# A decoder layer on one core: the first attention's sums turned in SBUF, GpSimd's bias work in pieces, stacks on every second partition

## The chip, the cores and the metric

The kernel runs on 1 core of a Trainium2 chip. The metric is the time of one execution on the device in microseconds (us).

## What is computed

The input is x, 16 batches of 128 tokens with 128 features, and a context of the same shape. Three blocks follow each other, each with a residual and a layer norm. Cut to what matters:

```python
# block 1: 16 heads of 8 features
scores = q @ k.T * SCALE                       # per head, 128x128
esc    = eq @ ek.T / sqrt(8) * exp(-0.1*|i-j|)  # the "entangled" scores
attn   = softmax(scores + 0.5 * esc)
ctx    = attn @ mixed                           # mixed: values with two gates
x = ln(x + ln(x + ctx @ Wo.T + bo) * g + b)
# block 2: cross attention on the context, 16 heads of 8, then layer norm
# block 3: 16 experts, top 4, GLU, then layer norm
```

## The kernel before

**Parts and stacks.** Projections are in float32. Each is split into three bfloat16 parts (`high`, `middle`, `lowest`; L1206 to L1217 on ScalarE, L494 to L506 on GpSimd, GpSimd forming the remainders). SyncE spills the parts of a batch to DRAM in five DMAs (`spill`, L348 to L374) and reads them back as stacks (`stack1`, L376 to L386; `stack2`, L388 to L397): a stack puts 6 parts times 8 features of every head on R = 48 partitions, so that one bfloat16 matmul over the 128 partitions of `stk` (the other rows are zeros from a memset at L484) sums all products of parts. `stack1` moves a batch in two halves of 8 heads, each half in one DMA.

**The first attention** goes in slots, one for each batch, with four units of four heads (g = 0 to 3) in a slot. In slot n the scores of batch n-1 are made, and the older batches n-2 to n-6 are at later steps; the remainders of batch n+2 are formed. TensorE's order in a unit is written out in `unit1` (L866): entangled scores (L753), at g = 1 and 3 the weighing of values (`weigh`, L838), the scores (L763), at g = 2 the projection of a later batch (L731), then for the unit before (lag 1) `subtract_max` (L768), for the one before that (lag 2) `turn` (L775), and at g = 1 `to_tokens` (L851).

One unit passes through these steps:

1. VectorE, `pick` (L1507): entangled scores times decay, PSUM to SBUF.
2. VectorE, `maximum` (L1517): four custom instructions add the picked scores to the scores, in place in PSUM (banks 0 and 1), and leave each row's maximum in `shift`.
3. TensorE, `subtract_max`: one 512-column bfloat16 matmul adds -shift to the bank.
4. ScalarE, `exponent` (L1219): exp, PSUM to `prob` in SBUF.
5. TensorE, `turn`: four float32 transposes of `prob` into bank 3.
6. ScalarE, `take_turned` (L1245): copy of bank 3 to `prob_t`.
7. TensorE, `weigh`.

**GpSimd** runs `slot1` (L582): `gain_and_sum` of batch n-5, the remainder of batch n+2, `inverse_root` for batch n-4, `mix_values` of batch n-1, `lowest` of batch n+2, `inverse_root` for batch n-5. Between the early slots it forms `xb_all` (x plus bo) and `xl_all` (x plus the norm's bias) in four additions each (`base`, L601, called at L619 to L628); VectorE waits for all four of `xb_all` at L1686, ahead of slot 4. Late in the first attention it forms the second block's `xb_all` in place (`residual_bias`, L636; 8, 4 and 4 batches).

**The overlap of the attentions.** From slot 14 on the projections and parts of the second attention are made (`begin2` on TensorE at L1007 and on ScalarE at L1375, `first_parts2` on GpSimd at L662), and from slot 17 the two attentions' units are interleaved until slot 20; then `slot2` runs alone. At (14, 0) ScalarE waits until the last spills of both buffers have landed (L1381).

**The start.** SyncE issues the weights, then `spill` and `stack1` of batches 0 and 1 with the load of `x_tok` (1 MB, L412) between the spill of batch 1 and its stack, then `late_w` and the further batches.

## Time and profile before

| | |
|---|---|
| median of 3 runs | 363.0 us (362.45 to 364.02) |
| the profiled execution's own time | 365.59 us |
| its span, first to last instruction | 363.8 us |
| mean granted clock of TensorE | 0.978 of full speed |
| first attention alone (slots 1 to 16) | about 18.9 to 159.5 us of the span |
| both attentions interleaved (slots 17 to 20) | to about 182 us |
| second attention alone | to about 265 us |
| experts and the last norm | to the end |
| busy shares | PE 91%, DVE 71%, ACT 60%, POOL 59% |
| DMA queue of SyncE | 67328 packets, 52.43 MB |

PE is TensorE's matmuls, PEld its weight loads, DVE is VectorE, ACT ScalarE, POOL GpSimd, SP SyncE; a letter q behind a name is its queue. Instructions overlap: the row of one gives its whole duration, while the next one on the same engine can start some 0.1 us before its end. So what one costs its engine is read from start to start.

### The profile page before, as it was taken

The numbers are of one execution on the slowest core, as the hardware profiler recorded it, in microseconds if no ns is written. First come the engines' busy times: TensorE is split into PE (matmuls) and PEld (weight loads), VectorE is DVE, ScalarE is ACT, GpSimd is POOL, SyncE is SP. The second block draws the span as 40 slices with busy tenths as digits, with TensorE's granted clock in tenths as the row PEclk, the third lists the DMA queues.
The fourth block names the chain that finished last, engine by engine and source line by source line (L and its number), as shares of the span: only waits on it lengthen the run. The fifth ranks groups of instructions, "written<-read, shape, count | busy, mean of one in ns | idle before, by whom it ended". The sixth has DMA issues, their size and how long they took to land.

```text
span 363.8 us, 11400 instructions
## 1 busy us (share of the span) xinstructions
PE 332.0 (91%) x3536; PEld 256.6 (71%) x3536; DVE 257.2 (71%) x1220; ACT 218.7 (60%) x522; POOL 215.0 (59%) x401
## 2 busy tenths in 40 slices
PE   8987989999999979896799999999799999999993
PEld 5766777877787758775678788888556765666662
DVE  1686888999999988875457776769945269345454
ACT  3785778999998866684586766756453252212120
POOL 8475789998888874876753334321125355464552
PEclk9998999999999998998899999999999999999998
DMA  7799899798998895947355757561046220444310
GB/s 232 174 304 239 220 235 238 177 208 200 196 208 186 208 204 107 255 95 150 76 126 106 156 127 140 126 138 46 2 136 202 77 60 0 142 128 131 128 32 29
DMA packets 67807, 54.06 MB, mean 149 GB/s; under 512 B 29616, under 2 KB 57648, under 8 KB 67632
## 3 DMA queue, kind: packets, MB, share of 16 engines
q1 hardware_dynamic: 67328, 52.43, 60.4%
q10 hardware_dynamic: 432, 1.05, 0.9%
q8 instruction: 24, 0.39, 0.5%
q14 instruction: 23, 0.19, 0.2%
HBM read 33.40 MB, written 20.05 MB: 147 GB/s over the span
## 4 chain that ended last, share of the span: by engine, by line
PE 51%; issue 13%; DVE 11%; ACT 9%; POOL 6%; DMA 5%; SPq 3%; ACTq 0%; POOLq 0%; DVEq 0%
PE bank L838 7%; PE bank L1106 5%; PE bank L1110 4%; PE bank L1119 4%; DMA parts_dram<-parts 3%; PE bank L792 3%; PE bank L821 3%; PE bank L814 3%; PE bank L731 3%; PE bank L781 3%; PE bank L763 2%; PE bank L771 2%; PE bank L851 2%; DMA stk<-parts_dram 2%; ACT parts L1217 2%
## 5 line engine op out<-in xcount | busy, mean ns | idle before, releaser
L1526 DVE CUSTOM_DVE_ANT_0 bank<-bank,decayed_e 128x128 f32<-128x128 f32 x256 | 67.2, 325 | 0.5
L697 POOL TENSOR_TENSOR stk<-stk 128x512 f32<-128x512 f32 x32 | 40.7, 1271 | 38.5 <-ACT stk L1442 35.8
L1537 DVE TENSOR_REDUCE top<-bank 128x4 bf16<-128x512 f32 x64 | 43.9, 687 | 19.5 <-PE bank L792 19.3
L1234 ACT ACTIVATE prob_t<-bank 128x512 f32<-128x512 f32 x64 | 38.8, 606 | 27.9 <-PE bank L821 27.6
L1442 ACT ACTIVATE stk<-bank 128x512 f32<-128x512 f32 x32 | 19.1, 597 | 53.6 <-PE bank L1106 53.6
L1781 DVE TENSOR_TENSOR stk<-bank,stk 128x512 f32<-128x512 f32 x32 | 22.0, 691 | 39.1 <-POOL stk L697 38.0
L1224 ACT ACTIVATE prob<-bank 128x512 f32<-128x512 f32 x64 | 39.2, 613 | 16.3 <-PE bank L771 16.0
L838 PE MATMUL bank<-prob_t,vmix 128*32 128x128 f32 x1024 | 43.6, 283 | 5.5 <-ACT pvs L1258 5.5
L1514 DVE TENSOR_TENSOR decayed_e<-bank,decay 128x512 f32<-128x512 f32 x64 | 44.0, 688 | 4.4 <-issue 4.3
L499 POOL TENSOR_TENSOR rest<-pf,parts 128x256 f32<-128x256 f32 (+1 forms) x31 | 28.1, 906 | 27.7 <-ACT parts L1213 27.7
L505 POOL TENSOR_TENSOR parts<-rest,parts 128x256 bf16<-128x256 f32 (+1 forms) x31 | 28.1, 906 | 25.9 <-ACT parts L1217 25.9
L781 PE MATMUL bank<-ident,prob 128*128 128x128 f32 x256 | 39.7, 279 | 0.0
L1250 ACT COPY prob_t<-bank 128x512 f32<-128x512 f32 x64 | 38.3, 599 | 0.9 <-PE bank L781 0.7
L1526 DVE DVE_READ_ACCUMULATOR2_ANT shift<- 128x1 bf16 x256 | 37.1, 145 | 0.1
L781 PEld LDWEIGHTS bank<-ident,prob 128*128 128x128 f32 x256 | 31.1, 143 | 6.5 <-issue 2.4
L838 PEld LDWEIGHTS bank<-prob_t,vmix 128*32 128x32 f32 x1024 | 26.4, 111 | 13.0 <-issue 7.8
L1119 PEld LDWEIGHTS bank<-w,stk 128*128 128x128 f32 x192 | 25.1, 191 | 11.9 <-issue 8.4
L1106 PE MATMUL bank<-x_t,w 128*128 128x512 f32 x64 | 32.8, 595 | 0.0
L1110 PE MATMUL bank<-x_t,w 128*128 128x512 f32 x64 | 32.7, 592 | 0.0
L753 PE MATMUL bank<-stk 128*128 128x128 bf16 x256 | 25.2, 222 | 3.4 <-DMA stk<-parts_dram 2.8
L763 PE MATMUL bank<-stk 128*128 128x128 bf16 x256 | 25.2, 221 | 2.3 <-ACT prob L1224 2.2
L771 PE MATMUL bank<-shift,neg_ident 128*128 128x512 bf16 x64 | 24.9, 389 | 2.1 <-DVE shift L1526 1.9
(172 smaller groups left out, 781.1 us busy)
## 6 DMA issues: line engine op xcount, KB each, us to landing
stk<-parts_dram SPq DMA_DIRECT2D x32, 384.0 KB, 5.4
stk<-shares_dram SPq DMA_DIRECT2D x64, 128.0 KB, 3.0
parts_dram<-parts SPq DMA_DIRECT2D x32, 192.0 KB, 3.1
parts_dram<-parts SPq DMA_DIRECT2D x48, 128.0 KB, 2.8
stk<-parts_dram SPq DMA_DIRECT2D x32, 192.0 KB, 3.5
parts_dram<-parts SPq DMA_DIRECT2D x32, 96.0 KB, 2.9
parts_dram<-parts SPq DMA_DIRECT2D x48, 64.0 KB, 2.1
w<-in_w_dram SPq DMA_DIRECT2D x3, 512.0 KB, 5.5
```

The source lines that it names most:

```text
L697: pool.tensor_tensor(h1[kk % 2], sg[kk % 2], share[kk], ALU.mult).then_inc(weighted, 1)
L781: t = pe.transpose(bank[3][:, 128 * j:128 * j + 128], prob[g % 2][:, j, :], ident[:])
L838: w = pe.matmul(bank[4][32 * j:32 * j + 32, 128 * m:128 * m + 128], vmix[b.par][:, head(2 * m, j) // 2, e:e + 2, :].rearrange("p e f -> p ...
L1106: pe.matmul(bank[kk % 2][:], w1[:, 128 * kk:128 * kk + 128], xt, start=True, stop=True).then_inc(gate_mm, 1)
L1110: pe.matmul(bank[UP_BANK[u % 3]][:], w3[:, 128 * kk:128 * kk + 128], xt, start=True, stop=True).then_inc(up_mm, 1)
L1119: m = pe.matmul(bank[4 + c % 2][:, 128 * t:128 * t + 128], actt[u % 3][:, 128 * t:128 * t + 128], w2[:, kk, :], start=(kk == 0 and t == 0) ...
L1224: act.activation(prob[g % 2][:].rearrange("p h t -> p (h t)"), bank[g % 2][:], ACT.Exp).then_inc(L.exped, 1)
L1234: act.activation(prob_t[g][:].rearrange("p h t -> p (h t)"), bank[2 + g % 2][:], ACT.Exp).then_inc(L2.exped, 1)
L1250: act.copy(prob_t[g][:].rearrange("p h t -> p (h t)"), bank[3][:]).then_inc(L.turned_ev, 1)
L1514: dve.tensor_tensor(decayed_e[:, g % 2], bank[E_BANK[g % 2]][:].rearrange("p (h t) -> p h t", h=GH), decay[:].unsqueeze(1).broadcast_to([1 ...
L1526: m = dve.tensor_tensor_reduce(out=bank[g % 2][:, 128 * j:128 * j + 128], in0=bank[g % 2][:, 128 * j:128 * j + 128], in1=decayed_e[:, g % ...
L1537: dve.tensor_reduce(top[:, b.par, GH * g:GH * g + GH], bank[S2_BANK[g % 2]][:].rearrange("p (h t) -> p h t", h=GH), AX.X, ALU.max).then_in ...
```

## The change

1. `maximum` writes its sums to SBUF (`sums`) and no longer back to the bank. `turn` transposes the sums (float32) into bank 3 and adds -shift there with four 128-column bfloat16 matmuls; it runs at lag 1. ScalarE's `exponent` reads bank 3 and writes `prob_t`. `subtract_max`, `take_turned` and `prob` are gone. Scores now wait for `maxed` and no longer for `exped`.
2. `residual_bias` goes in four pieces of 4 batches, and the parts of the second attention's first four batches are formed inside GpSimd's slots 14 to 17 (`last_slot1`). The `base` additions are spread over slots 2 to 7, and VectorE waits for the first of them ahead of slot 4 and for all four ahead of slot 6.
3. ScalarE's wait at (14, 0) for both spill buffers is replaced by one for the buffer in question ahead of `high` in slots 14 and 15. One wait of TensorE (L1078) is dropped.
4. The 48 rows of each stack lie on partitions 0, 2, ..., 94 in place of 0 to 47.
5. The load of `x_tok` is issued after both halves of batch 1's stack.

```diff
-        prob = [sb(f"prob{p}", [128, GH, S]) for p in range(2)]
+        sums = [sb(f"sums{p}", [128, GH, S]) for p in range(2)]
...
-                sp.dma_start(dst[0:R, :, at:at + H // 2], src[:, :, at:at + H // 2]
+                sp.dma_start(dst[0:2 * R:2, :, at:at + H // 2], src[:, :, at:at + H // 2]
...
-                    sp.dma_start(stk2[b.buf][0:R, side], src[side]).then_inc(L2.stacked[b.buf], 16)
+                    sp.dma_start(stk2[b.buf][0:2 * R:2, side], src[side]).then_inc(L2.stacked[b.buf], 16)
...
             spill(L1, Batch(0, 1))
-            sp.dma_start(x_tok[:].rearrange("p b n -> p (b n)"), k["x_tok"]).then_inc(in_xt, 16)
             sp.wait_ge(zeroed[1], 1)
             stack1(Batch(0, 1), 0)
             spill(L1, Batch(1, 0))
             stack1(Batch(0, 1), 1)
+            sp.dma_start(x_tok[:].rearrange("p b n -> p (b n)"), k["x_tok"]).then_inc(in_xt, 16)
...
+            pool.wait_ge(dve_set, DV_END)
+            slot1(1, 0)
             pool.wait_ge(in_tail_rows, 16)
             pool.wait_ge(in_xt, 16)
-            pool.wait_ge(dve_set, DV_END)
             base(xb_all, bo1, 0, base_x)
-            slot1(1, 0)
             base(xb_all, bo1, 1, base_x)
+            slot1(1, 1)
             base(xb_all, bo1, 2, base_x)
-            slot1(1, 1)
             base(xb_all, bo1, 3, base_x)
+            slot1(2, 0)
             base(xl_all, ln_b, 0, base_b)
-            slot1(2, 0)
-            for c in range(1, 4):
-                base(xl_all, ln_b, c, base_b)
+            pool.wait_ge(base_b, 1)
+            slot1(2, 1)
+            base(xl_all, ln_b, 1, base_b)
+            slot1(3, 0)
+            base(xl_all, ln_b, 2, base_b)
+            slot1(3, 1)
+            base(xl_all, ln_b, 3, base_b)
             pool.wait_ge(base_b, 4)
-            slot1(2, 1)
-            pair1(3)
...
+            def last_slot1(n, parts):
+
+                b = Batch(n // 2, n % 2)
+                if b.back(5).live:
+                    gain_and_sum(b.back(5))
+                if b.back(4).live:
+                    inverse_root(b.back(4), 0)
+                if parts is not None:
+                    remainder(L2, parts)
+                if b.back(1).live:
+                    mix_values(b.back(1))
+                if b.back(5).live:
+                    inverse_root(b.back(5), 1)
+                if parts is not None:
+                    lowest(L2, parts)
+
             pool.wait_ge(L1.low, NB)
-            first_parts2(0)
-            slot1(7, 1)
-            residual_bias(0, 8)
-            first_parts2(1)
-            slot1(8, 0)
-            first_parts2(2)
-            slot1(8, 1)
-            slot2(slot_batch(0))
-            slot1(9, 0)
+            for n in range(14, 17):
+                last_slot1(n, Batch2(0, n - 14))
+            last_slot1(17, Batch2(0, 3))
+            residual_bias(0, 4)
+            last_slot1(18, None)
             slot2(slot_batch(1))
+            residual_bias(4, 8)
+            last_slot1(19, None)
+            slot2(slot_batch(2))
             residual_bias(8, 12)
-            slot1(9, 1)
-            slot2(slot_batch(2))
-            slot1(10, 0)
+            last_slot1(20, None)
             slot2(slot_batch(3))
             residual_bias(12, NB)
...
-                    pe.wait_ge(L1.exped, u - 1)
+                    pe.wait_ge(L1.maxed, u - 1)
...
-            def subtract_max(b, g):
+            def turn(b, g):
+
                 u = b.n * NG + g
                 pe.wait_ge(L1.maxed, u + 1)
-                pe.matmul(bank[g % 2][:].rearrange("p (h t) -> p h t", h=GH), neg_ident[:],
-                          shift[:, g % 2, :].unsqueeze(2).broadcast_to([128, GH, S]),
-                          start=False, stop=True, skip_group_check=True).then_inc(L1.shifted, 1)
-
-            def turn(b, g):
-                u = b.n * NG + g
-                pe.wait_ge(L1.exped, u + 1)
                 if not isinstance(u, int) or u >= 1:
-                    pe.wait_ge(L1.turned_ev, u)
+                    pe.wait_ge(L1.exped, u)
                 for j in range(GH):
-                    t = pe.transpose(bank[3][:, 128 * j:128 * j + 128], prob[g % 2][:, j, :], ident[:])
-                t.then_inc(L1.turned, 1)
+                    pe.matmul(bank[3][:, 128 * j:128 * j + 128], sums[g % 2][:, j, :], ident[:], start=(j == 0), stop=True,
+                              is_transpose=True, skip_group_check=True)
+                for j in range(GH):
+                    m = pe.matmul(bank[3][:, 128 * j:128 * j + 128], shift[:, g % 2, j:j + 1].broadcast_to([128, 128]),
+                                  neg_ident[:], start=False, stop=True, skip_group_check=True)
+                m.then_inc(L1.turned, 1)
...
-                    if (n, g) == (NB + 1, 2):
-                        pe.wait_ge(L1.exped, NG * NB)
...
+            def exponent(b, g):
                 u = b.n * NG + g
-                act.wait_ge(L.shifted, u + 1)
-                if not isinstance(u, int) or u >= 2:
-                    act.wait_ge(L.turned, u - 1)
-                act.activation(prob[g % 2][:].rearrange("p h t -> p (h t)"), bank[g % 2][:], ACT.Exp
-                               ).then_inc(L.exped, 1)
+                act.wait_ge(L1.turned, u + 1)
+                if not isinstance(u, int) or u >= 4:
+                    act.wait_ge(L1.pv, b.n * NM + g // 2 - 1)
+                act.activation(prob_t[g][:].rearrange("p h t -> p (h t)"), bank[3][:], ACT.Exp).then_inc(L1.exped, 1)
...
-                    for p in range(2):
-                        act.wait_ge(L1.spilled[p], NB // 2 * L1.spill_step)
...
                     if g == 1:
+                        if b.n < 2:
+                            act.wait_ge(L1.spilled[b.par], NB // 2 * L1.spill_step)
                         high(L2, b, False)
...
-                            out=bank[g % 2][:, 128 * j:128 * j + 128], in0=bank[g % 2][:, 128 * j:128 * j + 128],
+                            out=sums[g % 2][:, j, :], in0=bank[g % 2][:, 128 * j:128 * j + 128],
...
             pair1(1)
+            dve.wait_ge(base_x, 1)
+            pair1(2)
             dve.wait_ge(base_x, 4)
-            pair1(2)
...
-            dve.wait_ge(xb2, 3)
+            dve.wait_ge(xb2, 4)
```

## Rows read from the trace of the kernel before

**Rows 1.** Busy time by stage: stretch, length, busy PE, PEld, DVE, ACT, POOL, clock, DMA share, GB/s.
```profile
60.00:80.00 20.00, 19.22 (x242) 15.89 (x239) 19.17 (x130) 17.48 (x43) 18.57 (x46) 1.00 0.89 203
...
160.00:180.00 20.00, 14.88 (x163) 12.16 (x163) 10.22 (x34) 12.08 (x33) 14.91 (x40) 0.84 0.57 113
...
182.00:265.50 83.50, 80.08 (x1278) 66.41 (x1278) 61.00 (x190) 55.30 (x148) 25.93 (x52) 1.00 0.50 106
...
265.50:363.80 98.30, 90.88 (x461) 58.12 (x460) 50.91 (x146) 26.51 (x44) 46.53 (x40) 0.99 0.32 98
```
**Rows 2.** Chain that ended last, one slot of the first attention: start, us, what.
```profile
81.40 0.43 ACT pvs L1258
...
81.97 0.67 PE bank L838 x16
...
82.97 0.21 PE bank L771
...
83.18 0.44 PE bank L781 x4
...
84.06 0.50 PE bank L731 x4
```
**Rows 3.** The same chain in the second attention: the subtraction in its existing form there.
```profile
181.12 0.22 PE bank L821 x4
```
**Rows 4.** Timeline of VectorE: first `pick` of five slots, then a values addition and slot 17's first.
```profile
27.93 0.69 DVE L1514 TENSOR_TENSOR decayed_e<-bank,decay 128x512 f32<-128x512 f32 x1 [0.32 <-issue]
...
47.91 0.69 DVE L1514 TENSOR_TENSOR decayed_e<-bank,decay 128x512 f32<-128x512 f32 x1 [1.27 <-issue]
...
80.56 0.69 DVE L1514 TENSOR_TENSOR decayed_e<-bank,decay 128x512 f32<-128x512 f32 x1
...
88.23 0.69 DVE L1514 TENSOR_TENSOR decayed_e<-bank,decay 128x512 f32<-128x512 f32 x1
...
112.71 0.69 DVE L1514 TENSOR_TENSOR decayed_e<-bank,decay 128x512 f32<-128x512 f32 x1
...
157.39 0.67 DVE L1676 TENSOR_TENSOR v_all<-bank,rows 128x512 f32<-128x512 f32 x1
...
159.67 0.29 DVE L1594 TENSOR_TENSOR res<-bank,xb_all 128x128 f32<-128x128 f32 x1
```
**Rows 5.** Timeline of GpSimd: one operation in two successive slots, then the bias additions.
```profile
74.22 0.46 POOL L570 TENSOR_TENSOR gained<-centred,rows 128x128 f32<-128x128 f32 x1
...
81.85 0.46 POOL L570 TENSOR_TENSOR gained<-centred,rows 128x128 f32<-128x128 f32 x1
...
55.40 3.74 POOL L603 TENSOR_TENSOR xl_all<-x_tok,rows 128x512 f32<-128x512 f32 x3
...
149.16 2.37 POOL L639 TENSOR_TENSOR xb_all<-x_tok,rows 128x1024 f32<-128x1024 f32 x1
...
173.75 1.26 POOL L639 TENSOR_TENSOR xb_all<-x_tok,rows 128x512 f32<-128x512 f32 x1
```
**Rows 6.** Timeline of ScalarE: start, us, line, what, [idle before <-releaser].
```profile
88.09 0.59 ACT L1250 COPY prob_t<-bank 128x512 f32<-128x512 f32 x1
...
134.71 0.37 ACT L1195 ACTIVATE pf<-bank,bias_q 128x128 f32<-128x128 f32 x1 [3.09 <-DMA parts_dram<-parts]
...
152.18 0.41 ACT L1217 CAST parts<-rest 128x256 bf16<-128x256 f32 x1 [2.11 <-POOL rest L499]
```
**Rows 7.** DMA issues of the page: size of one issue and us to landing.
```profile
stk<-parts_dram SPq DMA_DIRECT2D x32, 384.0 KB, 5.4
```
**Rows 8.** Busy time in two stretches of 1 us, columns as in rows 1.
```profile
73.00:74.00 1.00, 0.55 (x14) 0.40 (x15) 1.00 (x11) 1.00 (x5) 0.92 (x4) 1.00 0.99 160
...
76.00:77.00 1.00, 1.00 (x13) 0.98 (x12) 1.00 (x8) 0.60 (x2) 0.92 (x4) 1.00 1.16 343
```
**Rows 9.** Start of the kernel: the x_tok issue of SyncE.
```profile
17.04 0.55 SPq L412 DMA_DIRECT2D x_tok<-in_x_tok_dram  x1
```
**Rows 10.** Start of the kernel: the chain's step from the spill just before it.
```profile
16.45 5.66 DMA parts_dram<-parts
```

44 lines of the change are left out of this document (13 added, 31 removed).

## The prediction

> **What bounds the kernel now.** I read the busy time by stage first. The second attention keeps TensorE busy 80.08 of 83.5 us, and the experts take another 98.30 us [rows 1]. No edit touches what bounds these two stages, so I carry them over unchanged. The first attention is where four engines and the DMA queues are all near full: in 60 to 80 us TensorE 19.22, VectorE 19.17, GpSimd 18.57, ScalarE 17.48 of 20 us, and the DMA share is 0.89 [rows 1]. Where all are full, the busy share doesn't say which one ends last, so the chain of waits comes next. In a slot it runs half through ScalarE: its copy of `pvs` at 81.40 releases the weighing at 81.97 [rows 2], and ScalarE is late there because all its exponents and copies of that slot are in line before it.
>
> Third, the timelines give each engine's own length of a slot when nothing holds it. VectorE goes from 80.56 to 88.23, 7.67 us, in its best slot; four slots took 112.71 - 80.56 = 32.15, or 8.04 each [rows 4]. GpSimd repeats after 81.85 - 74.22 = 7.63 us of uninterrupted work [rows 5]. TensorE: eight groups of scores at 0.22 (the form of [rows 3]), four subtractions at 0.21, four turns at 0.44, two weighings at 0.67, two projections at 0.50 [rows 2], and five single float32 operations at a quarter of a turn (0.11): 7.3 us. So a slot can fall from 8.04 to 7.67 and no further, however much ScalarE sheds. The larger sums lie at the ends: slots 2 and 3 took 47.91 - 27.93 = 19.98 us and slots 12 to 16 took 159.67 - 112.71 = 46.96, 9.4 each [rows 4].
>
> **The change, part by part.**
>
> **Sums turned in SBUF.** ScalarE loses the copy of every unit: 64 times 0.59 [rows 6], 2.4 us of a slot at most (a little less, since starts overlap). That takes it from the chain: it falls under 6 us of a slot. TensorE swaps one 512-column subtraction (0.21) for four of 128 columns; the same form stands in the second attention at 0.22 for four [rows 3], so I take nothing; worst case the four cost their weight loads openly, which that row excludes. VectorE's write goes to SBUF in place of PSUM. No row has that custom instruction with the other target; I take no change. Bounds: the two ends are nothing and 0.05 us each way for an instruction, 0.8 us of a slot. The nearest row is the values addition, 0.67 for 512 elements from PSUM to SBUF against 0.69 for `pick` [rows 4]: such targets go at the usual rate, hence zero.
>
> The wait on `maxed` stood at the same place in TensorE's queue (lag 1) already; what is new is that the four transposes are behind it too, and behind them the next unit's entangled scores, a weighing or projection, and scores. VectorE meanwhile has one whole unit (7.67 / 4 = 1.92 us) in hand. TensorE needs 0.44 + 0.22 for the turn, 0.22 + 0.67 + 0.22 for the rest, 1.77 us, and the last 0.22 is wanted only after VectorE's next `pick`. So VectorE isn't starved. Bank 3 is now a single buffer: turn 0.66, exponent 0.59, about 0.1 for semaphores, 1.35 us, below 1.92.
>
> Steady slots then go at VectorE's pace with GpSimd 0.04 us behind it. I take 7.8. Slots 8 to 11: 4 x (8.04 - 7.8) = **-0.9 us** (ends -1.5 and 0).
>
> **Stack rows and the token load.** A slot moves 768 KB of spill and 768 KB of stack. At 0.89 of 8.04 us that is 7.2 us of all queues. The two kinds differ: with a stack in flight a stretch shows 160 GB/s at a share of 0.99, with spills 343 at 1.16 [rows 8]. So spills take about 2.3 us of a slot and stacks 4.9; together 7.2, as found. The slow kind is the one that lands on 48 adjacent partitions. Bounds for a stack after the change: 2.3 (the spill's rate) and 4.9 (nothing gained), with a loss as a rival below. I take 3.0, nearer the spill, since bytes and run length are alike and only the landing side differs. By the Trainium skill (SBUF, State Buffer, section "Door 1: The DMA port swizzle") partitions 0 to 47 reach 8 of 16 ports and load half of these twice, while 0, 2, ..., 94 reach all 16 with at most four rows on each; worked out from that, an estimate of half the time, 2.4 us. The trace agrees in direction with 160 against 343 [rows 8].
>
> At the start this counts. The spill of batch 1 took 5.66 us to land [rows 10] with the 1 MB of `x_tok` issued right behind it at 17.04 [rows 9]; at 343 GB/s that load alone is 3.1 us, and it sat ahead of both stacks of batch 1. One half stack has 5.4 us to landing [rows 7]. From the first stack's issue on (12.7 us, some 4 us ahead of `x_tok`), slots 2 to 4 need three spills (6.9), 3.5 stacks (17.2 now, 10.5 after), `x_tok` and `late_w` (4.1): the data for slot 4 is there at 40.9 now and 34.2 after, plus 2 to 5 us of latency. VectorE alone would need some 7 us for each of slots 2 and 3 (7.67 less the norm steps that they don't have, an estimate). It waits 1.27 us for the last `xb_all` piece ahead of slot 4 [rows 4]; with the new wait on one piece that goes. I take 14.5 for 19.98: **-5.5 us** (ends -6.0 and -2.5). `x_tok` itself is wanted later now, since GpSimd starts its bias work one slot later; the load collides with batch 2's spill, whose stack has some 5 us to spare.
>
> **Bias work of the start.** Eight additions of 1.25 us stay. Before, three stood in a row at 55.40 for 3.74 us [rows 5]. Now slots 5, 6 and 7 carry one each: GpSimd needs 7.63 + 1.25 = 8.9 us there against VectorE's 7.67, less some 1.5 us of slack. Slots 4 to 7 took 80.56 - 47.91 = 32.65. VectorE's floor is 30.7, GpSimd's surplus adds about 1.9: **0 us** (ends -1.9 and +2).
>
> **ScalarE's wait and the bias in pieces.** ScalarE stood 3.09 us at 134.71 for the last spill [rows 6]; now only `high` of slot 15 asks for that spill, a slot later, when it has long landed. Gone. At 149.16 GpSimd ran eight batches of bias, 2.37 us, and ScalarE waited 2.11 us for the remainder behind it [rows 5, 6]. Now the remainder goes inside the slot. VectorE's floor for slots 12 to 16 is 5 x 7.67 plus four additions of values at 0.6 (0.67 with the overlap off) [rows 4], 40.8. With 1.2 us left for what is late next (the remainder behind GpSimd's root, which itself waits for VectorE): 42.0 for 46.96, **-5.0 us** (ends -6.2 and -3).
>
> **Slots 17 to 20.** 22.3 us to 182, with TensorE busy 14.88 of 20 and a clock of 0.84 [rows 1]: chains through GpSimd, not load. Two 1.26 us pieces more fall here than before [rows 5], +2.5 if each is on the chain; the shorter pipeline (one lag less) and parts formed earlier give about as much. **0** (ends -2.5 and +2.5). The dropped wait of TensorE is nothing: exponents are done by then.
>
> **Sum:** -5.5 + 0 - 0.9 - 5.0 + 0 = -11.4 us. The profiled execution took 365.59, so 354.2 on its own scale; it lies 2.6 above the median of 363.0, and on the median's scale I predict **351.6 us**.
>
> **The rivals.**
>
> *B, the stack's rate stays.* Then DMA needs 7.2 us of every slot, and 1 MB of `c_t` more in slots 3 to 6 puts these at 8.5 and over. For: the share is above 1 through the start as it is, and nothing in the trace shows what holds the stack back; reading from DRAM would do it too. The Trainium skill says in the same page (section "A bandwidth-pool intuition that's wrong") that HBM is almost always the end-to-end bottleneck, by which the landing side would matter little. Against: 343 GB/s with spills [rows 8], though these write DRAM. Slots 2 and 3 lose 1.7 of the gain, slots 4 to 7 some 1.8 more: **355 us**.
>
> *C, GpSimd takes ScalarE's place.* Its 7.63 has no slack against 7.67, and it waits for VectorE and ScalarE in every slot. Then slots 4 to 7 rise 2, slots 8 to 11 stay, 12 to 16 give 4.1, 17 to 20 cost 2.4: -5.2, **358 us**.
>
> *D, slower.* Rows on every second partition make a stack dearer. It decides from 5.7 us on (2.3 + 5.7 = 8.0, the slot of now); two landings of 5.4 one after the other [rows 7] would be the far end. At a third more (6.5) a slot takes 8.8: twelve slots times 0.76 is +9.1, ScalarE's wait gives back 3.1: **369 us**. Against: same issues, same runs, same number of rows.
>
> *E, nothing reaches the end*, what is gained is waited for ahead of the second attention: 363.
>
> **How the numbers follow.** Forecast 0.55, B 0.22, C 0.14, D 0.06, E 0.03. All favourable ends of the forecast sum to about -17, so the low end is 346.5; B and most of C lie under 359: that leaves out D, E and a tail on each side, near 0.2. About 0.5% (1.8 us) is what a measurement of this kernel can tell from no change. Faster than 361.2: forecast, B and C less a tail, 0.89; same 0.05; slower 0.06. The forecast's own range is 347 to 356.
>
> **What would show it.** Right: slots 8 to 11 at 7.7 to 7.9 us with VectorE without idle time; the DMA share of 60 to 80 us down to 0.7 or less at a higher or equal GB/s (still 0.89 or more: B); slot 4's first `pick` near 42; no wait of ScalarE for a spill in slot 14; slots 12 to 16 in 42 us. GpSimd as the releaser of VectorE's `stats` in slots 5 to 8 and a slot of 8 us would be C. Wrong altogether if TensorE waits for `exped` at bank 3, or if the second attention's 83.5 us change.

## The result and the profile after

The kernel after takes 357.41 us at the median of 4 runs (356.22 to 358.72) against 362.86 for the kernel before: a ratio of 0.9846, 95% interval 0.9804 to 0.9887. That is 5.45 us less. The forecast was 11.4 less, to 351.6; the range 346.5 to 359.0 holds the time, its middle doesn't. The profiled execution took 357.19 us with a span of 355.4, where the one before took 365.59 with 363.8: on that scale the change looks like 8.4 us. Why 8.4 and 5.45 differ is part of what follows.

Busy time by stage of the kernel after, columns as in [rows 1]. The last two stretches are those of [rows 1] moved by 8.4 us, so their lengths are chosen and not measured:

```profile
60.00:80.00 20.00, 19.18 (x274) 16.89 (x273) 18.47 (x133) 14.27 (x38) 18.75 (x42) 1.00 0.78 230
160.00:180.00 20.00, 13.85 (x216) 11.75 (x216) 10.43 (x30) 12.14 (x32) 15.47 (x37) 1.00 0.54 135
173.60:257.10 83.50, 78.78 (x1249) 65.39 (x1250) 61.15 (x191) 53.80 (x142) 26.01 (x52) 1.00 0.42 104
257.10:355.40 98.30, 90.88 (x461) 58.13 (x460) 50.86 (x146) 26.51 (x44) 46.64 (x40) 0.98 0.30 98
```

ScalarE lost 3.2 us of 20, and the queues are down from 0.89 to 0.78 at more GB/s. Whether the late stages kept their length is read from VectorE's `top`, a reduction that only the second attention has. Its first and its last start, in the timeline of the kernel before and then of the kernel after:

```profile
163.19 0.66 DVE L1537 TENSOR_REDUCE top<-bank 128x4 bf16<-128x512 f32 x1
258.71 0.69 DVE L1537 TENSOR_REDUCE top<-bank 128x4 bf16<-128x512 f32 x1
```

```profile
155.51 0.66 DVE L1529 TENSOR_REDUCE top<-bank 128x4 bf16<-128x512 f32 x1
250.31 0.69 DVE L1529 TENSOR_REDUCE top<-bank 128x4 bf16<-128x512 f32 x1
```

They lie 95.52 us apart before and 94.80 after, and the last one starts 105.09 us ahead of the end of the span in both. So the experts are unchanged and the second attention is unchanged within 0.7 us.

The half stack and VectorE's custom instruction, from the issues and the groups of the page of after (KB and us to landing; busy us and mean ns):

```profile
stk<-parts_dram SPq DMA_DIRECT2D x32, 384.0 KB, 4.3
...
L1518 DVE CUSTOM_DVE_ANT_0 sums<-bank,decayed_e 128x128 f32<-128x128 f32 x256 | 59.1, 287 | 0.7
```

The landing was 5.4 in [rows 7]. Timeline of VectorE in the kernel after, the starts that answer to [rows 4] (slots 2, 4, 8, 12, the last `pick` of slot 16, and slot 17's first instruction):

```profile
28.75 0.69 DVE L1506 TENSOR_TENSOR decayed_e<-bank,decay 128x512 f32<-128x512 f32 x1
44.88 0.69 DVE L1506 TENSOR_TENSOR decayed_e<-bank,decay 128x512 f32<-128x512 f32 x1
77.37 0.69 DVE L1506 TENSOR_TENSOR decayed_e<-bank,decay 128x512 f32<-128x512 f32 x1
110.13 0.69 DVE L1506 TENSOR_TENSOR decayed_e<-bank,decay 128x512 f32<-128x512 f32 x1
150.50 0.69 DVE L1506 TENSOR_TENSOR decayed_e<-bank,decay 128x512 f32<-128x512 f32 x1
152.09 0.29 DVE L1586 TENSOR_TENSOR res<-bank,xb_all 128x128 f32<-128x128 f32 x1
```

Read as in the prediction, from slot 12's first `pick` to slot 17's first instruction, slots 12 to 16 went from 46.96 to 152.09 - 110.13 = 41.96 us, the forecast's 42.0. Slots 4 to 7 went from 32.65 to 32.49, forecast 32.65. But slots 8 to 11 went from 32.15 to 32.76 where 31.2 was forecast, and slots 2 and 3 from 19.98 to 16.13 where it was 14.5.

The 64 `pick`s of the first attention turned out to be a ruler that hardly moves between executions, so every profile below is read with it. The table gives the us between the first `pick`s of slots; "12-16" ends at the last `pick` of slot 16, "tail" runs from there to the end of the span.

| kernel | first `pick` | 2-3 | 4-7 | 8-11 | 12-16 | tail | span |
|---|---|---|---|---|---|---|---|
| before | 18.94 | 19.98 | 32.65 | 32.15 | 45.26 | 205.83 | 363.8 |
| before_again | 20.66 | 16.81 | 32.66 | 32.15 | 45.61 | 205.83 | 362.9 |
| before_gp_unrolled | 19.36 | 18.30 | 32.67 | 32.16 | 43.36 | 206.94 | 361.9 |
| wait_only | 20.44 | 16.74 | 32.67 | 32.19 | 41.68 | 204.90 | 357.8 |
| rows_only | 18.98 | 16.72 | 32.67 | 32.18 | 42.99 | 207.57 | 360.3 |
| sums_old | 18.18 | 15.82 | 33.14 | 32.96 | 40.40 | 205.92 | 355.6 |
| after | 19.63 | 16.13 | 32.49 | 32.76 | 40.37 | 204.90 | 355.4 |
| after_again | 18.39 | 16.21 | 32.80 | 32.66 | 40.38 | 205.23 | 354.8 |
| rows_adjacent | 18.28 | 18.16 | 34.04 | 32.69 | 40.47 | 205.24 | 358.0 |
| xtok_old_place | 17.91 | 15.44 | 32.49 | 32.75 | 40.38 | 205.20 | 353.3 |
| old_wait | 18.32 | 16.81 | 32.67 | 32.84 | 44.05 | 205.89 | 359.7 |
| old_bias | 18.63 | 16.42 | 32.47 | 32.79 | 41.25 | 205.72 | 356.4 |
| bias_out | 20.72 | 15.44 | 32.49 | 32.75 | 40.38 | 206.40 | 357.3 |
| pv_first | 18.67 | 16.08 | 32.50 | 33.32 | 40.28 | 205.62 | 355.6 |
| gp_unrolled | 19.13 | 15.89 | 32.47 | 32.06 | 40.54 | 207.89 | 357.1 |
| bases_later | 20.37 | 15.43 | 32.47 | 31.38 | 40.54 | 206.09 | 355.4 |
| two_bounds | 18.52 | 17.40 | 31.28 | 30.29 | 40.51 | 205.68 | 352.8 |
| two_bounds_again | 18.71 | 15.56 | 31.26 | 30.28 | 40.52 | 205.55 | 351.0 |

Three columns vary with nothing edited in them: the first `pick` by up to 2.8 us, slots 2 and 3, and the tail. Slots 12 to 16 vary in the kernels that have the old wait (42.99 to 45.61), for a reason shown below. Slots 4 to 7 and 8 to 11 repeat within 0.31 us for one kernel, and mostly within 0.1. Every row is one execution, while the medians come from 4 to 12.

### The profile page after: what moved, and what is told of

Read it like the earlier page. It is cut to its first block, busy times and chain, and to the rows that moved or that the text cites. A ratio compares the mean times of both kernels' runs of the same rounds, so it can differ in the third digit from the quotient of the medians.

```text
span 355.4 us, 11656 instructions
## 1 busy us (share of the span) xinstructions
PE 326.9 (92%) x3728; PEld 259.1 (73%) x3728; DVE 250.7 (71%) x1220; ACT 190.7 (54%) x458; POOL 215.4 (61%) x402
## 4 chain that ended last, share of the span: by engine, by line
PE 45%; POOL 16%; issue 11%; DVE 9%; DMA 9%; ACT 4%; SPq 4%; POOLq 0%; ACTq 0%; DVEq 0%
PE bank L844 6%; PE bank L1109 5%; DMA parts_dram<-parts 4%; PE bank L1113 4%; PE bank L784 4%; PE bank L1122 4%; DMA stk<-parts_dram 2%; PE bank L773 2%; POOL rstd L562 2%; PE bank L799 2%; POOL rest L498 2%; DMA sup_w<-in_sup_w_dram 2%; PE bank L828 2%; PE bank L821 2%; PE bank L787 2%
## 5 line engine op out<-in xcount | busy, mean ns | idle before, releaser
L1227 ACT ACTIVATE prob_t<-bank 128x512 f32<-128x512 f32 x64 | 38.7, 605 | 41.6 <-PE bank L787 41.6
L1518 DVE CUSTOM_DVE_ANT_0 sums<-bank,decayed_e 128x128 f32<-128x128 f32 x256 | 59.1, 287 | 0.7
L1236 ACT ACTIVATE prob_t<-bank 128x512 f32<-128x512 f32 x64 | 38.8, 606 | 26.7 <-PE bank L828 26.3
L844 PE MATMUL bank<-prob_t,vmix 128*32 128x128 f32 x1024 | 42.6, 278 | 2.2 <-ACT pvs L1253 2.2
L784 PE MATMUL bank<-ident,sums 128*128 128x128 f32 x256 | 39.3, 276 | 2.7 <-ACT prob_t L1227 1.2
L1113 PE MATMUL bank<-x_t,w 128*128 128x512 f32 x64 | 32.7, 592 | 0.0
L784 PEld LDWEIGHTS bank<-ident,sums 128*128 128x128 f32 x256 | 28.0, 141 | 5.8 <-DVE shift L1518 3.5
L763 PE MATMUL bank<-stk 128*128 128x128 bf16 x256 | 24.8, 219 | 1.2 <-DMA stk<-parts_dram 1.2
L1122 PE MATMUL bank<-w,stk 128*128 128x128 f32 x192 | 25.4, 275 | 0.0
L799 PE MATMUL bank<-stk 128*128 128x128 bf16 x256 | 24.9, 220 | 0.4 <-DVE top L1529 0.4
L773 PE MATMUL bank<-stk 128*128 128x128 bf16 x256 | 25.0, 220 | 0.0
L821 PE MATMUL bank<-stk 128*128 128x128 bf16 x256 | 24.8, 219 | 0.0
```

The lines of the kernel that those rows point to most:

```text
L784: pe.matmul(bank[3][:, 128 * j:128 * j + 128], sums[g % 2][:, j, :], ident[:], start=(j == 0), stop=True, is_transpose=True, skip_group_ch ...
L844: w = pe.matmul(bank[4][32 * j:32 * j + 32, 128 * m:128 * m + 128], vmix[b.par][:, head(2 * m, j) // 2, e:e + 2, :].rearrange("p e f -> p ...
L1113: pe.matmul(bank[UP_BANK[u % 3]][:], w3[:, 128 * kk:128 * kk + 128], xt, start=True, stop=True).then_inc(up_mm, 1)
L1122: m = pe.matmul(bank[4 + c % 2][:, 128 * t:128 * t + 128], actt[u % 3][:, 128 * t:128 * t + 128], w2[:, kk, :], start=(kk == 0 and t == 0) ...
L1227: act.activation(prob_t[g][:].rearrange("p h t -> p (h t)"), bank[3][:], ACT.Exp).then_inc(L1.exped, 1)
L1236: act.activation(prob_t[g][:].rearrange("p h t -> p (h t)"), bank[2 + g % 2][:], ACT.Exp).then_inc(L2.exped, 1)
```

## Experiments

### What each part of the change is worth

The kernel before again, to see how large its own spread is:

> The kernel before, unchanged, for a second trace. Theory V (the profiled execution of before was a slow one: 365.6 against its median of 362.9, mean clock 0.978): the new trace has a span near 361 and the stage that is shorter is the one after the DMA stall of slot 2, where TensorE fell to the 1.2 GHz level between 34 and 38 us, or the one after ScalarE's 3.1 us wait in slot 14. Rival W (the profile only adds time evenly): the same stages as in the first trace, slots 2 and 3 again 20 us and slots 12 to 16 again 47 us. Ratio to before 1.00.

Measured 362.44 us, ratio 1.0005 (0.9976 to 1.0034). Slots 2 and 3 took 16.81 us here and 19.98 in the profile that the forecast used. So theory V holds for the start, but not for slots 12 to 16, which took 45.61 us again. Part of the 19.98 is the clock. TensorE had waited 1.85 us for a stack until 32.51, and then (busy time in the columns of [rows 1], the kernel before and then before_again):

```profile
34.00:38.00 4.00, 4.00 (x37) 3.01 (x37) 1.99 (x14) 1.98 (x4) 1.57 (x2) 0.61 1.03 287
```

```profile
34.00:38.00 4.00, 3.94 (x50) 3.10 (x49) 3.50 (x22) 3.13 (x8) 3.31 (x7) 1.00 0.96 279
```

In before_gp_unrolled the wait for that stack was 1.42 us, the clock stayed at 1.00, and slot 2 took 9.01 us in place of 10.68. In before_again there was no such wait, and slot 2 took 7.51.

**ScalarE's wait.** Put back into the kernel after, and taken alone out of the kernel before:

```diff
@@ old_wait: the kernel after @@
                 if (n, g) == (14, 0):
                     act.wait_ge(L1.rest, NB)
+                    for p in range(2):
+                        act.wait_ge(L1.spilled[p], NB // 2 * L1.spill_step)
...
-                        if b.n < 2:
-                            act.wait_ge(L1.spilled[b.par], NB // 2 * L1.spill_step)
                         high(L2, b, False)
```

> The kernel after with ScalarE's two waits for the last spills back ahead of its first work for the second attention. Theory I: in the kernel before this wait held ScalarE 2.7 to 3.1 us, TensorE behind it, and in two of three profiles the clock fell to half for the next 3 to 4 us; slots 12 to 16 go from 40.4 to 42 or 44, median 359 to 361. Rival M: GpSimd and ScalarE are earlier here, the spill has landed or nearly, under 1 us: 357.5.

> The kernel before with one edit: ScalarE's two waits for the last spills moved from the head of slot 14's second-attention work to the writes that need them. Theory I: it gives what putting the wait back took, the slot of 11.84 us becomes 8.4 and slots 12 to 16 go from 45.3 to 41.9 us, median 3.4 us under the kernel before: 359.1. Rival B: in the old order the remainder behind the 2.37 us bias piece is late too, and takes the wait's place: 43.5 us, median 361.

old_wait: 360.04 us, ratio 0.9884 (0.9798 to 0.9971), slot 14 12.11 us in place of 8.48. wait_only (the same lines, the other way round, in the kernel before): 359.32 us, ratio 0.9901 (0.9866 to 0.9935), slot 14 8.30 in place of 11.84. This one edit gives 4.0 us by the medians where the whole change gives 5.45; put back, it costs 2.6 by the medians and 3.7 by the ruler. Timeline of ScalarE in old_wait, then of TensorE, and the chain of old_wait behind them, in order of time:

```profile
131.68 0.37 ACT L1198 ACTIVATE pf<-bank,bias_q 128x128 f32<-128x128 f32 x1 [3.34 <-DMA parts_dram<-parts]
```

```profile
132.94 0.63 PE L784 MATMUL bank<-ident,sums 128*128 128x128 f32 x4 [2.24 <-ACT prob_t L1227]
```

```profile
127.14 4.39 DMA parts_dram<-parts
...
133.79 1.69 PE bank L1007 x8
...
135.91 1.03 PE bank L844 x16
...
140.54 0.59 PE bank L844 x16
...
143.76 0.95 PE bank L1007 x8
```

ScalarE stands 3.34 us for the landing of the last spill, TensorE behind it has nothing to do for 2.24 us, and when it goes on, its instructions soon take nearly twice their time: 1.69 us for eight matmuls that take 0.95 a few us later, 1.03 for a weighing of 0.59. The granted clock of 120 to 140 us is 0.91 in old_wait, as in both profiles of the kernel before, and 1.00 in the kernel after. Two stretches of old_wait:

```profile
135.00:137.00 2.00, 2.00 (x25) 1.36 (x24) 1.30 (x3) 0.00 (x0) 1.76 (x6) 0.50 0.00 0
...
120.00:140.00 20.00, 17.53 (x224) 15.24 (x223) 15.54 (x106) 9.17 (x23) 13.39 (x36) 0.91 0.58 171
```

So part of the wait's price is the lower of the clock's two levels (1.2 for 2.4 GHz) right after TensorE stood idle. In before_gp_unrolled ScalarE's wait was 2.7 us, the clock stayed at 1.00, and slot 14 took 9.98 us for the 11.84 and 12.19 of the two profiles of before. Less the 0.4 us by which the wait itself was shorter, that puts some 1.5 us of the 3.7 on the clock, an estimate from single executions. rows_only is a second case without the fall: a wait of 2.3 us, clock 1.00, slot 14 at 9.61.

**GpSimd's order at the end.** The kernel after, with second-attention parts after each slot's own work and eight batches of bias in one piece, as before:

```diff
@@ old_bias: the kernel after, GpSimd @@
-            for n in range(14, 17):
-                last_slot1(n, Batch2(0, n - 14))
+            slot1(7, 0)
+            first_parts2(0)
+            slot1(7, 1)
+            residual_bias(0, 8)
+            first_parts2(1)
...
```

> The kernel after with GpSimd's order from slot 14 on as it was: second attention's parts after the slot's own work, the bias of batches 0 to 7 as one piece of 2.37 us after slot 15. Theory I: ScalarE waits again for the remainder behind it, 1.5 to 2.5 us in slots 15 and 16 (40.4 to 42.4), and the tail is 1 us shorter for one piece less: median 358.5. Rival M: the pieces behind slots 17 to 19 cost in the tail what this saves, no change, 357.4.

358.85 us, ratio 0.9889 (0.9808 to 0.9969): slot 16 takes 7.75 in place of 6.86, the tail 205.72. ScalarE waits for the remainder again, as in [rows 6] (2.11 us there). Timeline of ScalarE in old_bias:

```profile
144.96 0.41 ACT L1212 CAST parts<-rest 128x256 bf16<-128x256 f32 x1 [1.71 <-POOL rest L498]
```

The bias order is worth 0.9 us by the ruler and 1.4 by the medians, whose intervals overlap the kernel after's.

**Rows on every second partition**, undone in the kernel after and done alone in the kernel before:

```diff
@@ rows_adjacent: the kernel after @@
-                sp.dma_start(dst[0:2 * R:2, :, at:at + H // 2], src[:, :, at:at + H // 2]
+                sp.dma_start(dst[0:R, :, at:at + H // 2], src[:, :, at:at + H // 2]
```

> The changed kernel with the 48 rows of each stack back on partitions 0 to 47. Theory R (adjacent rows make a stack slower to land): DMA share of 60 to 80 us rises from 0.78 to 0.89 or more, half a stack takes 5.4 us in place of 4.3 to land, slots 2 to 6 wait for stacks, 2 to 4 us more, median 360. Rival S (the spread changes the queues' share but nothing that ends last, since slots 5 to 8 are GpSimd's and later ones TensorE's and ScalarE's): share up, time within 0.5 us.

> The kernel before with one edit: stack rows on every second partition. Theory I: slots 2 and 3 fall from 16.8 to 20.0 (three profiles) to 15.5 to 16.5, slots 4 to 7 and 8 to 11 stay (32.66, 32.15, set by compute), the landing of a 384 KB half stack from 5.4 to 4.3 us; median 360.2, 2.2 us under before, as the undo in the kernel after cost 2.2. Rival X: with x_tok still ahead of batch 1's stacks the queues stay full there, and it gives under 1 us.

rows_adjacent: 359.6 us, ratio 0.9915 (0.9879 to 0.9951), 2.2 us dearer than the kernel after, though the intervals just overlap. rows_only: 361.72 us, ratio 0.9962 (0.9930 to 0.9993), 1.6 us gained. The landing of a half stack from the page of rows_adjacent, then of rows_only:

```profile
stk<-parts_dram SPq DMA_DIRECT2D x32, 384.0 KB, 5.7
```

```profile
stk<-parts_dram SPq DMA_DIRECT2D x32, 384.0 KB, 4.2
```

Busy time by stage of rows_only, whose slots 4 to 7 are as long as the kernel before's, so that the share can be set beside [rows 1]:

```profile
60.00:80.00 20.00, 18.92 (x239) 15.51 (x238) 19.26 (x131) 18.46 (x48) 18.34 (x45) 1.00 0.70 201
```

201 GB/s for 203, at a share of 0.70 for 0.89; in the kernel after it is 0.78 at 230 GB/s, in rows_adjacent 0.97 at 235. By the forecast's own division that is 0.70 x 8.04 = 5.6 us of all queues a slot, less 2.3 for the spills 3.3 for the stacks, where it took 3.0 and had 4.9 before. The Trainium skill (SBUF, State Buffer, section "Door 1: The DMA port swizzle") has bandwidth follow the number of ports that the partitions reach, here all 16 for 8; the estimate from it was 2.4, and the measured third off agrees in direction and not in full.

In the kernel before the queues are no bound once slot 4 is reached: rows_only has 32.67 and 32.18 there, to 0.03 us the old values. In the kernel after they would be one for a slot more. rows_adjacent takes 2.0 us longer in slots 2 and 3 and 1.5 us longer in slot 4 (9.39 for 7.92). TensorE's timeline there:

```profile
50.32 0.40 PE L763 MATMUL bank<-stk 128*128 128x128 bf16 x4 [1.15 <-DMA stk<-parts_dram]
```

At the start the gain has a floor. In the profile of the kernel before TensorE waited 1.9 us in 28 to 48 us for a stack to land; in rows_only it waits for none, and slots 2 and 3 take 16.72 us. But before_again and wait_only, with adjacent rows, don't wait for one there either, and take 16.81 and 16.74. So the rows help where a stack happens to be late, and rows_only's one profile doesn't show where its 1.6 us come from.

**The later token load**, undone in the kernel after:

```diff
@@ xtok_old_place: the kernel after, SyncE @@
             spill(L1, Batch(0, 1))
+            sp.dma_start(x_tok[:].rearrange("p b n -> p (b n)"), k["x_tok"]).then_inc(in_xt, 16)
...
-            sp.dma_start(x_tok[:].rearrange("p b n -> p (b n)"), k["x_tok"]).then_inc(in_xt, 16)
             sp.dma_start(late_w[:], k["late_w"]).then_inc(in_late, 16)
```

> The changed kernel with the token load back between the spill of batch 1 and its stack. Theory T (the load is paid wherever it stands among the first stacks: 3 us of queue time): slot 2 waits again for its second half, slot 3's wait of 1 us and the 8.3 us landing of its first half stack go; slot 4 starts within 1 us of 44.9, median within 1 us of 357.4. Rival U (the later place is worth its whole 3 us, as I predicted): slot 4 starts at 47 to 48, median 360.

356.49 us, ratio 0.9843 (0.9799 to 0.9888): nothing lost. Slots 2 and 3 took 15.44 us, but bases_later and bias_out, which load late, took 15.43 and 15.44, with no wait for a stack. These two had their first `pick` latest, though: slot 4 starts at 42.5 us in xtok_old_place, at 44.9 and 45.3 in these two, and at 44.9 in the kernel after. In the kernel after the late load only moved the collision. Its chain around slot 3:

```profile
25.25 3.54 DMA parts_dram<-parts
28.80 0.02 issue
28.81 8.32 DMA stk<-parts_dram
```

SyncE issued `x_tok` at 26.41 us, so the half stack behind it needed 8.32 us where the page's median is 4.3.

**The turned sums**, left out: the kernel before with all the other parts, so that of the diff these hunks are missing:

```diff
@@ sums_old lacks, for one @@
-        prob = [sb(f"prob{p}", [128, GH, S]) for p in range(2)]
+        sums = [sb(f"sums{p}", [128, GH, S]) for p in range(2)]
...
-                            out=bank[g % 2][:, 128 * j:128 * j + 128], in0=bank[g % 2][:, 128 * j:128 * j + 128],
+                            out=sums[g % 2][:, j, :], in0=bank[g % 2][:, 128 * j:128 * j + 128],
```

> The kernel before with every part of the change but the first: rows on every second partition, the later token load, the bias work in pieces, ScalarE's waits moved; the sums stay in PSUM, with the copy of every unit on ScalarE. Theory I: the gain of slots 2 and 3 belongs to the rows and that of slots 12 to 16 to the waits, so these are 15.6 and 42.5 us here, slots 4 to 7 and 8 to 11 as before (32.7, 32.2), median 358.8. Rival A: without its 2.4 us off, ScalarE (14 to 17 of 20 us busy with the parts of the second attention added) is what ends slots 12 to 16 again: 44 us or more, median 360.5.

358.89 us, ratio 0.9890 (0.9809 to 0.9971). Slots 12 to 16 took 40.40 us, the same as with turned sums: ScalarE's copies didn't lengthen them once the waits were gone. Theory I was wrong in its 42.5, and rival A in its 44. Theory I was also wrong in slots 4 to 7 and 8 to 11: not 32.7 and 32.2 as before but 33.14 and 32.96, so the other parts of the change make these slots longer. From there the sums take 0.65 us in slots 4 to 7 and 0.2 in slots 8 to 11. By the medians they are worth 1.5 us, with intervals that overlap the kernel after's. The largest part of the diff is one of its smaller parts in time.

### Why slots 8 to 11 did not fall

The forecast had them at VectorE's 7.67 us each, with GpSimd at 7.63 from [rows 5] beside it. What came out is two things. Slot 8 alone went from 7.67 to 8.69 us, and slots 9 to 11 fell only from 24.48 to 24.07. In slot 8 the chain of the kernel after runs through the last of GpSimd's `xl_all` pieces. It stands behind slot 7 in GpSimd's program, but starts 2.3 us after slot 8's first `pick` at 77.37, and delays the sum that VectorE and TensorE then wait for:

```profile
79.67 1.24 POOL xl_all L602
...
81.85 0.45 POOL res L573
...
84.25 0.21 DVE attn_o L1608
84.50 0.33 PE bank L866
```

The turned sums aren't to blame: slot 8 is 8.96 us in sums_old, and 7.52 in bases_later below, which moves the pieces. The forecast had counted the pieces against slots 4 to 7 only.

In slots 9 to 11 two dependency loops were longer than 7.67. Chain of waits of the kernel after, one slot of it (start, us, what):

```profile
94.33 0.07 ACT pf L1201
...
94.58 0.38 ACT pf L1204
94.96 0.26 ACT pf L1206
95.22 0.27 ACT pvs L1253
95.49 0.14 issue
95.62 0.67 PE bank L844 x16
```

The copy of `pvs` still stands behind the four projection copies, and the weighing waits for it as in [rows 2]. The change took the copies of the turned exponents off ScalarE, but `pvs` kept its place, and from one weighing to the next (87.63 to 95.62) the chain is 7.99 us long. First trial: ScalarE takes `pvs` first.

```diff
@@ pv_first: the kernel after, ScalarE's unit1 @@
-                if g == 0 and bb.back(3).live:
-                    take_pv(L1, bb.back(3))
...
                     exponent(ub, ug)
+                if g == 3 and bb.back(2).live:
+                    take_pv(L1, bb.back(2))
```

> The changed kernel with ScalarE's copy of pvs moved ahead of the four projection copies (end of the slot before). Theory P (in slots 9 to 12 the slot is a loop TensorE turn - exponent - four projection copies - pvs copy - weighing, 2.06 us through ScalarE for 1.55 us of TensorE's own work): these slots fall from 8.15 to 7.7 us, the kernel gains 2 us, median 355.4. Rival Q (VectorE or GpSimd set the pace, the chain through ScalarE only looks so): slots stay at 8.1 or more, 357.4. Slots 5 to 8 keep their 8.7 us by both, because GpSimd sets them.

357.45 us, ratio 0.9856 (0.9825 to 0.9887), and slots 8 to 11 even took 33.32. TensorE no longer waits for `pvs`; the timelines of pv_first, VectorE and then TensorE, name what it waits for now:

```profile
98.01 0.29 DVE L1596 BATCH_NORM_STATS2 stats<-res 128x6 f32<-128x128 f32 x1 [0.94 <-POOL res L573]
...
100.19 0.33 PE L866 MATMUL bank<-ident,attn_o 128*128 128x128 f32 x1 [0.25 <-DVE attn_o L1608]
```

GpSimd is late with a sum, VectorE with `attn_o` behind it, and TensorE with the transpose of `attn_o`. So GpSimd's own slot was next. Its timeline in the kernel after, the same operation in four slots:

```profile
94.65 1.17 POOL L504 TENSOR_TENSOR parts<-rest,parts 128x512 bf16<-128x512 f32 x1
102.89 1.16 POOL L504 TENSOR_TENSOR parts<-rest,parts 128x512 bf16<-128x512 f32 x1
110.78 1.16 POOL L504 TENSOR_TENSOR parts<-rest,parts 128x512 bf16<-128x512 f32 x1
118.31 1.16 POOL L504 TENSOR_TENSOR parts<-rest,parts 128x512 bf16<-128x512 f32 x1
```

8.24, 7.89, then 7.53 us (and 7.89 for the turn before these). Slots 8 to 11 are a loop in GpSimd's program, and the next ones are written out. In the loop it stands 0.2 to 0.3 us ahead of two or three instructions of a slot, put down to its own instruction before or to issue. [rows 5] were read in the written-out part (74.22 to 81.85 us) and carried over into the loop. Three trials:

```diff
@@ gp_unrolled (kernel after), before_gp_unrolled (kernel before) @@
-            with pool.Fori(4, 6) as p:
+            for p in range(4, 6):
                 pair1(p)
@@ bases_later: the kernel after (and its waits on base_x and base_b to match) @@
 xb_all piece 3: behind slot 14 instead of slot 3
 xl_all piece 1: behind slot 7 instead of slot 5
 xl_all piece 2: behind slot 12 instead of slot 6
 xl_all piece 3: behind slot 15 instead of slot 7
```

> The kernel after, with GpSimd's loop over batches 8 to 11 written out. Theory G: GpSimd sets slots 8 to 11. Its turn is 8.24 and 7.89 us inside the loop (parts write to parts write, 94.65, 102.89, 110.78) and 7.53 us in straight code (110.78 to 118.31); so these four slots fall from 32.8 us to 31.0 (between 30.6 and 31.6), VectorE's last pick 1.7 us earlier, and the median goes from 357.4 to about 355.7. Rival T: TensorE sets them (busy 7.8 of 8.08 us, of which 7.5 is distinct issue time); then they stay at 32.4 or more. Rival K: unrolled code must be fetched, GpSimd shows new gaps, the slots get longer.

> The kernel before, with the same GpSimd loop written out. Theory G: here too it was GpSimd, not ScalarE, that set slots 8 to 11 (32.15 us in both profiles): they fall to 31.3 or less and the time by about 0.8 us. Rival S (the reading of the prediction: the chain ran through ScalarE's pvs copy): nothing moves, 32.1 us again, median 362.5.

> The kernel after, with three of GpSimd's eight bias pieces (1.25 us each) taken out of slots 3 to 7: one to slot 12, two behind slots 14 and 15, where TensorE sets the pace at 8.45 us. Theory G: GpSimd sets slots 5 to 8 (turns of 8.75 us); slots 4 to 7 go from 32.5 to 31.3 us and slot 8 from 8.69 to 8.1, 1.8 us in all, and slots 12 to 16 give back at most 0.5: median 356.1. Rival T: TensorE, 96 per cent busy there, sets them: slots 4 to 7 at 32.3 or more, no gain. Rival L: the pieces in slots 14 and 15 delay the norms and cost over 1 us there: 357.4 or more.

Each falls short of its theory. gp_unrolled: GpSimd's three turns of 7.89, 8.24 and 7.89 became 7.49, 7.51 and 7.51, but slots 8 to 11 took 32.06 for 32.76 where 31.0 was expected, median 357.51. bases_later: slots 8 to 11 at 31.38, but slots 4 to 7 still 32.47, to 0.02 us the old value, and median 357.61; in the profiled execution a later first `pick` (20.37) and a longer tail (206.09) took back what the slots gave. before_gp_unrolled: 363.07 us, ratio 1.0004, slots 8 to 11 at 32.16. So in the kernel before GpSimd's loop was not the bound. That fits the prediction's reading of ScalarE, which rests on the chain alone: no run moved `pvs` in the kernel before. In the kernel after, theory G was half of the cause. What was left is two loops of nearly equal length, 8.0 us through ScalarE and 7.9 to 8.2 through GpSimd (8.75 in slots 5 to 7, with a piece in each), each hiding what the other gives. The test is all three edits at once, those of pv_first, gp_unrolled and bases_later, with nothing else:

> The kernel after with three edits together: ScalarE takes pvs ahead of the four projection copies, GpSimd's loop is written out, three of its bias pieces come later. Theory W: in slots 4 to 11 two loops of nearly the same length hold each other (TensorE's turn, exponent, projection copies, pvs, weighing: 8.0 us; GpSimd's turn of 8.1 to 8.7), so each edit alone gave at most 1.4 us; with both gone a slot is at VectorE's and TensorE's own 7.5 to 7.7: slots 4 to 7 31.0 us (32.5), slots 8 to 11 31.0 (32.8), 3.3 us in all, median 354.5. Rival T: TensorE alone is the pace (7.5 us of issue and what it loses between forms): 32.2 and 31.4, no more than bases_later had. Rival R: what is gained is waited for later, in the second attention, and the tail from the last pick on grows above 207.

> The same three edits as two_bounds. If its gain is what the slots show (31.3 + 30.3 for 32.5 + 32.8, 3.7 us), its median lies 3.0 to 3.7 us under after_again's on the same chip. If most is waited for again in the second attention, the difference is under 1.5 us while the slots are as short.

> The kernel after, unchanged. Ratio to before 0.984 to 0.986, 357.3 us. The profile: slots 4 to 7 32.5, 8 to 11 32.76, 12 to 16 40.4 again within 0.1 us; the first pick anywhere from 17.9 to 20.7 and slots 2 and 3 from 15.4 to 16.4, which is where its executions differ.

two_bounds 354.34 us, ratio 0.9766 (0.9680 to 0.9852). Measured again, with more executions: 353.76 us, ratio 0.9745 (0.9716 to 0.9775), beside after_again with 357.66 and 0.9846 (0.9814 to 0.9879) on the same chip. The intervals don't meet; it is 3.9 us faster than the kernel after and 9.5 faster than the kernel before, and the ruler gives 32.80 + 32.66 - 31.26 - 30.28 = 3.9. Theory W holds: the three edits alone gave at most 1.4 us in these slots and nothing clear of noise in the time. No run had two of the three, so how much each adds to the others isn't known. Two stretches of two_bounds_again as long as its slots 8 and 9, both 1.1 us behind these slots' first `pick`s, busy time in the columns of [rows 1]:

```profile
75.74:83.06 7.32, 7.26 (x106) 6.46 (x99) 7.21 (x56) 5.05 (x13) 6.85 (x14) 1.00 0.83 241
83.06:90.97 7.91, 7.91 (x116) 7.02 (x113) 7.38 (x56) 5.74 (x16) 7.36 (x19) 1.00 0.72 205
```

TensorE is busy in 15.17 of 15.23 us, and the chain of 80 to 96 us is TensorE's alone. GpSimd isn't far behind: it goes through four turns of 7.50 us there without a wait, where the slots take 7.57 on average.

### The two-engine stretch at the end, and what comes back later

```diff
@@ bias_out: the kernel after, GpSimd @@
 residual_bias(0, 4): behind slot 14 instead of slot 17
 residual_bias(4, 8): behind slot 15 instead of slot 18
 residual_bias(8, 12), (12, 16): one slot later each
```

> The kernel after, with the four pieces of the second bias moved: two from slots 17 to 19 to behind slots 14 and 15, and the other two a slot later each. Theory C2: slots 17 to 20 hang on GpSimd (the chain from 147 to 176 us is nearly all GpSimd, three pieces of 1.23 us on it); from the last pick to the end 205 us become about 203, and the time 355.4. Rival: what ends them is the length of the norm chain of the last batches, the pieces fill gaps in it, and nothing moves (within 0.6 us); or the piece of batches 8 to 11 comes too late for the second attention's residual and that waits.

358.26 us, ratio 0.9838 (0.9761 to 0.9915), tail 206.40: no gain. From its waits in 180 to 240 us:

```profile
DVE top L1530 <- POOL xb_all L641: 2.3, 1, 2.3
```

The last piece now starts later, and VectorE stands behind it once, 2.3 us. It is the rival that the expectation named.

In gp_unrolled, bias_out, before_gp_unrolled and rows_only the tail is 1.1 to 3.0 us longer than in the kernels they come from. Part of it can be seen. Timeline of gp_unrolled, in the second attention:

```profile
208.88 0.40 ACT L1216 CAST parts<-pf 128x256 bf16<-128x256 f32 x1 [0.71 <-DMA parts_dram<-parts]
209.36 0.67 POOL L498 TENSOR_TENSOR rest<-pf,parts 128x256 f32<-128x256 f32 x1 [2.81 <-ACT parts L1216]
209.50 0.19 PEld L870 LDWEIGHTS bank<-late_w,attn_ot 128*128 128x128 f32 x1 [1.03 <-ACT attn_ot L1261]
209.50 0.38 PE L870 MATMUL bank<-late_w,attn_ot 128*128 128x128 f32 x1 [0.86 <-ACT attn_ot L1261]
```

ScalarE waits for a spill to land, and TensorE stands behind it; these waits sum to 2.7 us in gp_unrolled, 3.4 in bias_out, 2.6 in before_gp_unrolled and 2.6 in rows_only, and to nothing in before, before_again and after, 0.4 in after_again. It isn't the whole account: old_bias has 1.6 us of them and a tail of 205.72. Which executions have it, and why, stays open: no run changed only that. Nor was it tried what sets the first `pick`, whose spread of 2.8 us is there with and without the change.

## Why the prediction was right and wrong

- **Slots 12 to 16, -5.0: right in size, and right in its main cause.** Putting the spill wait back costs 3.7 us of the ruler and the bias order 0.9. What the forecast didn't have is the clock's share of it (some 1.5 us, paid in three of the five profiles that have the wait), and that the turned sums add nothing here.
- **Slots 4 to 7, 0: right** (-0.16), though the reason given is half of it. With three pieces taken out the slots stayed at 32.47, and with `pvs` first at 32.50; with both they took 31.26. So GpSimd's surplus and ScalarE's queue each held them.
- **Slots 17 to 20, 0: right** within the spread: the tail is 204.90 and 205.23 for 205.83.
- **The second attention and the experts: unchanged, right.** From the first `top` to the last it is 94.80 us for 95.52, and from there to the end 105.09 in both.
- **Slots 8 to 11, -0.9: wrong, +0.6.** The step that failed is "Steady slots then go at VectorE's pace with GpSimd 0.04 us behind it". Slots 9 to 11 take 8.02 us each: GpSimd's slot is 7.53 written out and 8.01 on average in its loop, and `pvs` still stands behind the queue of projection copies, which the change doesn't touch. The copies that it removed were not what made ScalarE late: with them, in sums_old, slots 9 to 11 take 24.00 us, and 24.07 without. And slot 8 got a whole us longer by the bias piece that the sum had put at nothing there; that is more than the 0.6 by which the four slots rose. "A slot can fall from 8.04 to 7.67 and no further" was wrong as well: two_bounds_again averages 7.57 in these four slots and has one of 7.32. VectorE's shorter instruction (below) fits this, but no run tested it alone.
- **Slots 2 and 3, -5.5: wrong in size, and the main error.** Two things. "VectorE alone would need some 7 us for each" was too low: executions in which nothing waits for a stack need 15.43 us for the two, and no profile is below that. With the old bias order it is 16.7, since VectorE still waits 1.27 us for the last `xb_all` piece. That wait went as forecast, and it is the part of the term that is sure; in the kernel after some of it was lost again to the stack that the moved load delays. And 19.98 was no fit start. The four profiles of kernels with the old rows, load and bias order show 19.98, 16.81, 18.30 and 16.74; the one used lies 2.7 above the mean of the other three, and its whole time lay 2.6 above the median. Some 1.7 us of the excess are in slot 2, where the clock fell (10.68 for 9.01 us). The forecast measured its term against the long execution, and then took that gain off the median, which never held it. From 17.3 to the 16.1 and 16.2 of the two profiles of after, the term is worth about 1.1 us. The conversion "354.2 on its own scale, 351.6 on the median's" was sound only if the excess lay outside the change.

By the ruler, with the mean of before, before_again and before_gp_unrolled against the mean of after and after_again: -0.6 (first `pick`) - 2.2 (slots 2 and 3) + 0 + 0.6 - 4.4 (44.7 for 40.4) - 1.1 (tail 206.2 for 205.1) = -7.7 us. The medians say -5.45. The profiled executions of the kernels before lie 0.6 to 2.7 us above their medians and those of after 0.2 and 1.1 below, so the profiles overstate the change. With slots 2 and 3 at -1.1, and the first `pick` left out, the sum is -6.0; that is a choice of profiles, and how the 5.45 divide is known to about 1 us for each term.

The low end of the range has an error of its own: the favourable ends are -6.0, -1.9, -1.5, -6.2 and -2.5, which is -18.1 and not "about -17". It changed nothing here.

Of the rivals, B is out (the stacks went from 4.9 to 3.3 us), and D and E with it; the rule of the Trainium skill beside B (SBUF, State Buffer, section "A bandwidth-pool intuition that's wrong"), that HBM is nearly always the bound, isn't borne out by 0.89 to 0.70 from a landing side alone. Rival C said 358 us, nearest to the 357.4 measured, and it had GpSimd beside ScalarE right, with slots 8 to 11 staying. Its sum was luck all the same: it kept the -5.5 of slots 2 and 3, and made up for it with +2 in slots 4 to 7 and +2.4 in slots 17 to 20 that didn't come. The chances for faster (0.89) and the range did their work. The central value did not, because the term of slots 2 and 3 was taken near its good end from a long execution, and slots 8 to 11 gave nothing.

## What to carry to other kernels

When the same event recurs in a kernel, list its starts in every profile: stretches that repeat to 0.05 us can be argued to tenths, and those that vary by 3 us between executions can't give a term of 5 from one profile. When one profile lies above the median, find the stretch that is long before subtracting anything in it. Read an engine's own pace in the very stretch where it is to apply, looped or written out, and where several loops are within 5% of each other, expect little from shortening one (here 0 to 1.4 us, for 3.9 with all). Work that is put into some slots can end in the next one; count it there too.
